# Reordering the prelude of a selective-scan layer: exponentials and logarithms by pairs of batches, all of softplus ahead of the scans, and the output bias from a product with ones

## The reference

```python
x = layernorm(x)                               # 4 x 512 x 128
gate = sigmoid(x @ W2 + b2)                    # 256 channels
u = sigmoid(causal_conv4(x @ W1 + b1) + conv_b)
xp = u @ x_proj_w                              # 64 + 16 + 16 columns
delta = softplus(xp[:, :64] @ dt_proj_w + dt_proj_b)
for each of 16 states n:                       # one recurrence over 512 tokens each
    h = exp(delta * A[n]) * h + delta * u * B[n]
    y += h * C[n]
out = (y + u * D) * gate @ Wo + bo             # added to the layer's input
```

## Time and profile before

| | |
|---|---|
| runs | 1500.18, 1506.36, 1511.74 us; median 1506.36 |
| profiled execution | 1509.37 us, of which span 1507.1 us |
| granted TensorE clock, mean | 0.883 of full speed |
| PE busy | 1237.4 us (82%) |
| DVE busy | 1035.0 us (69%) |
| ACT busy | 729.2 us (48%) |
| POOL busy | 628.0 us (42%) |
| scan layer: prelude | 0 to 72.07 us, when the first scan starts |
| scan layer: scans and tail | 72.07 to 304.81 us |

### The profile page before, as it was taken

The page is one execution under the profiler, slowest core; times in us unless marked ns, Lnnn a source line. Parts: engine busy times, 40 slices in busy tenths (PEclk is TensorE's granted clock), DMA queues, the critical chain, the costliest instruction groups (busy, mean ns, idle before and its releaser), DMA issues. The chain is left out here.

```text
span 1507.1 us, 30851 instructions
## 1 busy us (share of the span) xinstructions
PE 1237.4 (82%) x11642; PEld 673.8 (45%) x11642; DVE 1035.0 (69%) x2290; ACT 729.2 (48%) x1596; POOL 628.0 (42%) x838
## 2 busy tenths in 40 slices
PE   6656677779999988538889988988988799999976
PEld 2212232222333337424666766666666333333276
DVE  6699999979888955457446646645632588988653
ACT  3834334317766675313524523533442166676754
POOL 2279888853424215314423423223332524351244
PEclk9878888869999998758889879978997599999988
DMA  5378833023224022441421231141120231331213
GB/s 166 145 274 320 298 139 140 20 67 87 55 65 122 13 82 63 100 86 23 88 38 25 45 74 28 21 100 18 18 51 10 67 79 31 97 89 45 81 48 88
DMA packets 137737, 128.41 MB, mean 85 GB/s; under 512 B 92007, under 2 KB 123559, under 8 KB 132202
## 3 DMA queue, kind: packets, MB, share of 16 engines
q1 hardware_dynamic: 129536, 118.56, 28.6%
q0 software_dynamic: 2496, 5.13, 1.1%
q10 hardware_dynamic: 5558, 2.76, 0.9%
HBM read 105.61 MB, written 38.62 MB: 96 GB/s over the span
## 5 line engine op out<-in xcount | busy, mean ns | idle before, releaser
L1393 DVE TENSOR_REDUCE f_row_min<-f_ps 128x1 f32<-128x512 f32 x512 | 323.9, 676 | 55.6 <-PE f_ps L1720 55.2
L1283 ACT ACTIVATE f_e<-f_ps 128x512 f32<-128x512 f32 x512 | 282.8, 602 | 126.4 <-PE f_ps L1740 122.5
L1720 PE MATMUL f_ps<-f_operands 72*128 72x512 bf16 x512 | 205.4, 410 | 26.4 <-DMA f_operands<-k_scr 15.4
L1740 PE MATMUL f_ps<-f_operands 75*128 75x512 bf16 x512 | 189.5, 380 | 2.6 <-ACT f_e L1283 2.1
L790 PE MATMUL m_ps<-m_shared,sb_ident 128*128 128x512 f32 x256 | 136.8, 683 | 58.1 <-DVE m_shared L630 58.0
L363 POOL TENSOR_TENSOR m_drive<-m_du,m_ring 128x1024 f32<-128x1024 f32 x64 | 149.7, 2352 | 56.2 <-DVE m_ps L622 37.6
L495 ACT ACTIVATE m_ps<-m_delta,m_A 128x511 f32<-128x511 f32 x128 | 83.0, 681 | 131.7 <-DVE m_ps L622 109.0
L1751 PE MATMUL f_ps<-f_e,f_v_op 128*32 128x512 f32 x1024 | 136.4, 604 | 2.1 <-ACT f_e L1283 1.4
L2714 DVE TENSOR_TENSOR d_aT<-d_ps,d_aT 128x16 f32<-128x16 f32 x224 | 37.9, 169 | 140.9 <-PE d_ps L2892 140.7
L1720 PEld LDWEIGHTS f_ps<-f_operands 72*128 72x128 bf16 x512 | 51.3, 101 | 181.2 <-DVE f_row_min L1393 127.3
L2545 DVE TENSOR_REDUCE d_row_min<-d_ps 128x1 f32<-128x384 f32 (+3 forms) x176 | 106.3, 634 | 35.9 <-PE d_ps L2786 34.7
(11 more groups left out here) (298 smaller groups left out, 2345.3 us busy)
## 6 DMA issues: line engine op xcount, KB each, us to landing
m_ring<-bc_scr SPq DMA_DIRECT2D x32, 1024.0 KB, 5.4
f_rows_scr<-blank SPq DMA_DIRECT2D x2, 8707.5 KB, 30.8
f_wall<-f_wall SPq DMA_DIRECT2D x16, 578.0 KB
f_operands<-q_scr SPq DMA_DIRECT2D x32, 288.0 KB
f_operands<-k_scr SPq DMA_DIRECT2D x96, 96.0 KB
d_q_op<-q_scr SPq DMA_DIRECT2D x6, 576.0 KB
d_k_op<-k_scr SPq DMA_DIRECT2D x18, 192.0 KB
f_operands<-f_rows_scr SPq DMA_DIRECT2D x46, 64.5 KB, 1.8
```

The source lines that it names most:

```text
L1283: nc.scalar.activation(e_sb[:, n % 3, hh, :], ps[:, SCORE[(b * UNITS + u) % SCORE_BANKS], :], ACT.Exp, scale=SCALE).then_inc(s["e_out"], 1)
L1393: nc.vector.tensor_reduce(row_min[:, b % 2, u // TPB, u % TPB:u % TPB + 1], ps[:, MAXQ[(b * UNITS + u) % MAX_BANKS], :], AX.X, ALU.max, ne ...
L1720: nc.tensor.matmul(ps[:, MAXQ[n % MAX_BANKS], :], q_op(b, QK)[:, hd, t * P:(t + 1) * P], k_op(b, QK)[:, hd, :], start=True, stop=True).the ...
L1740: nc.tensor.matmul(ps[:, SCORE[n % SCORE_BANKS], :], k_op(b, QKS)[:, hd, t * P:(t + 1) * P], q_op(b, QKS)[:, hd, :], start=True, stop=True ...
```

## The change

On ACT: `steps(0)` moves in front of `gates(1)`; `inputs(2)` and `steps(1)` come next; then the exponentials of batches 0 and 1 follow each other, then their logarithms; `inputs(3)`, `steps(2)`, `gates(2)`, `gates(3)`, `steps(3)`; the exponentials of 2 and 3, and their logarithms, all ahead of the first decay. On DVE `one_plus`, and then `softplus`, run by pairs too, and those of batches 2 and 3 stand in front of the scans. On PE `project_rows(1)` moves in front of `project_u(2)`, `project_dt(0)` in front of `project_gate(1)`, and likewise for the later batches. POOL's four additions of the bias go, with `add_output`'s wait for them; instead `project_out` opens each 128 x 128 tile of the sum with a product of a row of ones and the row `m_bo` (four more matmul calls a batch), for which DVE sets `ones_row` at the start.

```diff
-                pool.wait_ge(s["rest_in"], 16 * (1 + len(later_loads(core))))
-                for b in range(B):
...
-                    nc.gpsimd.tensor_tensor(x_sb[:, tiles, :], x_sb[:, tiles, :],
-                                            row(core, "m_bo").unsqueeze(1).to_broadcast([P, TPB, H]),
-                                            ALU.add).then_inc(s["bias_out"], 1)
...
                 inputs(1)
                 turned(2)
                 raw(2)
+                steps(0)
                 gates(1)
                 turned(3)
-                steps(0)
+                inputs(2)
+                steps(1)
                 decline(0)
+                decline(1)
                 logarithm(0)
-                inputs(2)
+                logarithm(1)
                 inputs(3)
-                steps(1)
+                steps(2)
                 gates(2)
                 gates(3)
-                decline(1)
-                steps(2)
-                logarithm(1)
                 steps(3)
                 decline(2)
                 decline(3)
+                logarithm(2)
+                logarithm(3)
...
-                        if step == DEFERRED_AT + 1:
-                            for later in DEFERRED:
-                                logarithm(later)
...
                 norm(3)
+                projections(1)
                 convolve(2)
-                projections(1)
+                projections(2)
                 one_plus(0)
+                one_plus(1)
                 softplus(0)
-                projections(2)
-                one_plus(1)
+                softplus(1)
                 projections(3)
-                softplus(1)
                 dve.wait_ge(s["gate_out"], B)
...
-                for later in DEFERRED:
-                    one_plus(later)
+                one_plus(2)
+                one_plus(3)
+                softplus(2)
+                softplus(3)
...
-                    dve.wait_ge(s["bias_out"], b + 1)
...
-                    if step + 1 == DEFERRED_AT:
-                        for later in DEFERRED:
-                            softplus(later)
...
                 turn(2)
+                project_rows(1)
                 project_u(2)
+                project_dt(0)
                 project_gate(1)
-                project_dt(0)
                 turn(3)
-                project_rows(1)
+                project_dt(1)
+                project_rows(2)
                 project_u(3)
-                project_dt(1)
+                project_dt(2)
                 project_gate(2)
-                project_rows(2)
+                project_rows(3)
                 project_gate(3)
-                project_dt(2)
-                project_rows(3)
                 project_dt(3)
...
                     for t in range(TPB):
+                        here = bank(Y)[:, t * H:(t + 1) * H]
+                        nc.tensor.matmul(here, ones_row[:, :], row(core, "m_bo")[0:1, :], start=True, stop=False)
```

More of the change, by code:

```diff
@@ L217, in mamba_phase @@
         CONV_STEPS = CONV_K * HALVES
-        DEFERRED = (2, 3)
-        DEFERRED_AT = 1
         gate = sb("gate", [P, HALVES, T])
@@ L232, in mamba_phase @@
         edge_w = sb("edge_w", [CONV_K - 1, MLP])
+        ones_row = sb("ones_row", [1, P])
         PAD = S + CONV_K - 1
@@ L260, in mamba_phase @@
                  "dt_ps z_out e_out one_e_out lost_out log_out log1p_out delta_out du_out decay_zeroed decay_out drive_out "
-                 "scan_out hC_dve_out hC_pool_out y_dve y_pool yg_out o_ps bias_out x_out "
+                 "scan_out hC_dve_out hC_pool_out y_dve y_pool yg_out o_ps ones_out x_out "
                  "f_stats f_mv f_var f_rstd f_hn f_hT_ps f_hT_sb f_qk_ps f_qk_sb f_split f_stored")
@@ L346, in _ @@
                     layer_norm_rstd(nc, pool, core, ln[b % 2], s, "ln", b + 1)
-                pool.wait_ge(s["rest_in"], 16 * (1 + len(later_loads(core))))
-                for b in range(B):
-                    tiles = slice(b * TPB, (b + 1) * TPB)
-                    pool.wait_ge(s["ln_done"], b + 1)
-                    nc.gpsimd.tensor_tensor(x_sb[:, tiles, :], x_sb[:, tiles, :],
-                                            row(core, "m_bo").unsqueeze(1).to_broadcast([P, TPB, H]),
-                                            ALU.add).then_inc(s["bias_out"], 1)
                 def drive_of(step):
@@ L517, in _ @@
                 nc.vector.memset(core.minus_half[:, :], -0.5)
+                nc.vector.memset(ones_row[:, :], 1.0).then_inc(s["ones_out"], 1)
                 for i in range(2):
@@ L797, in project_out @@
                         pe.wait_ge(s["rest_in"], 16 * (1 + len(later_loads(core))))
+                        pe.wait_ge(s["ones_out"], 1)
                     for t in range(TPB):
+                        here = bank(Y)[:, t * H:(t + 1) * H]
+                        nc.tensor.matmul(here, ones_row[:, :], row(core, "m_bo")[0:1, :], start=True, stop=False)
                         for k in range(HALVES):
-                            last = nc.tensor.matmul(bank(Y)[:, t * H:(t + 1) * H], yg[:, k, t * P:(t + 1) * P],
-                                                    Wo[:, k, :], start=(k == 0), stop=(k == HALVES - 1))
+                            last = nc.tensor.matmul(here, yg[:, k, t * P:(t + 1) * P], Wo[:, k, :], start=False, stop=(k == HALVES - 1))
                     last.then_inc(s["o_ps"], 1)
```

## The result

The changed kernel takes 1514.9 us (median of 20 runs, 1506.4 to 1522.1) against 1507.2 for the kernel before in 20 runs: ratio 1.0053, 95% interval 1.0036 to 1.0069. It is 8 us slower. I had forecast 1 us faster, and the range ended at 1511.

What follows compares the result with a forecast made beforehand. It took DVE as the bound from the first scan on, and a chain of hand-overs before it. Earlier scans -2.6, wait at first gating +0.6, product with ones +1.0: -1.0 us, 1505.3 against 1506.4; range 1498.5 to 1511.

Steps and rivals of the forecast that it cites:

- the product with ones: Bias added on PE by four more calls a batch: 1.0 us a batch, added whole only in the last batch.
- For batches 0 to 2 it is hidden: In these batches the longer product costs nothing, since `add_output` comes 4.8 us after the product ends.
- The ladder of the prelude: Six timed stages before the scans: scan 0 starts at 80.0, scan 2 at 85.7 in place of 88.29, 2.6 us gained.
- rival A's second half: PE at full clock at `project_dt(3)`, before 3.05 us: prelude 1.1 us shorter, 1500.6 with both halves; whole rival's chance 0.25.
- Step 4: In the prelude, `softplus(1)` on DVE takes turns with POOL's first four drives: 52.2 to 60.5 in place of 56.0.
- Step 2: In the prelude, POOL adds no bias: `norm(3)` ends at 32.6, not 35.49, `convolve(2)` at 38.9, not 41.25; gain 2.4.
- Chunk 8: Ring chunk on SP's queue behind the first blank copy: lands at 122.6 in place of 115.7; POOL waits 3.0 before drive 16.
- The wait at the gating: DVE's first gating, `gated(0)`, due at 132.9, waits 0.6 us for PE's sums, which end at 133.5.
- rival B's sign: A pause of DVE before `gated(0)` of over 2 us.
- Rival B: Slower: the ring chunk behind the blank copy lands 2 to 6 us later than 122.6, giving 1507 to 1511; chance 0.15.
- The sum: Whole kernel: -2.6 + 0.6 + 1.0 = -1.0 us, with the layer's end at about 304.
- the named slower rivals: Late ring chunk, 1507 to 1511, chance 0.15; PE losing its clock in the prelude, 1509, chance 0.05.

Runs made afterwards that it cites:

- e7b_ones_k64: The changed kernel with the product with ones over 64 rows in place of one; a single execution, only its trace read: last product 5.8 us.

## Why the prediction was wrong, point by point

**The step that failed is the product with ones.** "Four calls more are 1.0 us a batch if a contraction over one row costs what one over 128 does (the nearest row; the bounds are 0 and, at the half clock seen elsewhere, 2.0)". The sum for 128 rows was right: that run's last product took 2.94 us, 0.9 over 2.05. For one row the batch took 4.3 more than 2.05, not 1.0. Two things that I had not priced make the other 3.4: about 0.4 us a tile at the full clock for the changes between unlike numbers of rows (1.4 a batch, from the batch with 64 rows at the full clock), and the clock, which falls while PE works and slows the old sixteen instructions too (2.1). My upper bound took the half clock for the new instructions alone.

**"For batches 0 to 2 it is hidden"** failed for batch 2. I compared the product's end with `add_output` only. Behind it on PE stand the two products that make q and k of the next layer, ACT waits for them in its list, and its decays wait behind: 2.15 and 0.51 us of idle DVE. With 128 rows only the 0.51 is left.

**The ladder of the prelude held.** Scan 0 was to start at 80.0 and scan 2 at 85.7; it was 78.77 and 84.47. Of the 1.2 us, 1.1 are rival A's second half, the clock at `project_dt(3)`: 1.98 us, not 3.05. Step 4, the turns, held: `softplus(1)` took 7.8 us (52.42 to 60.22) where I had 8.3, and the run with later drives took 4.1 of them away. Step 2's bias off POOL is worth 2.9 in the new order and nothing in the old.

**Chunk 8** landed at 122.6 (93.82 and 28.8), the time that I had, but by luck: the blank copy was issued 1.2 us earlier than forecast (88.54), took 31.8 us in place of 30.3, and chunk 8 came 2.3 behind it. POOL, ready earlier too, paused 4.2, not 3.0. The wait at the gating was 3.5, not 0.6: the scans were 1.2 us ahead of my ladder and only waited for it, and the sums ahead of it ran partly at the lower clock (131 to 133 us at 0.63 and 0.50; 5.40 us where eight sums at the full clock take 3.70), which took them to 135.23 in place of 133.5. In six like runs where the clock held in these sums the wait was 1.0 to 1.4 us. So rival B's sign came, a pause of over 2 us, but not its cause: the chunk was on time. Rival B itself came in `e7b_ones_k64`: the blank copy took 33.3 us, chunk 8 landed at 124.8, and the gating waited 3.50 us with the clock at 1.00.

**The sum.** Against my forecast the layer ends 7.0 us late (310.84 for 303.8): 1.8 at the first gating (135.27 for 133.5), 3.3 in the last product beyond its 1.0, 2.6 in batch 3, and -0.7 at the two gatings between.

**The rivals' chances.** I gave the named slower rivals 0.2 in all, and none of it to the one part of the change that was new on the chip. I took the range for an operation that the trace did not show from rows of another shape, and gave it no rival. The trace of the kernel before had a nearer row, in the prelude, at the full clock:

```profile
41.28 0.38 PE L711 MATMUL m_ps<-sb_m_edge,m_edge_w 3*128 3x3 f32 x2
41.59 3.70 PE L710 MATMUL m_ps<-m_shared 128*128 128x512 f32 x8
```

Two instructions over 3 rows and with 3 columns each, among products over 128 rows, take 0.31 us from start to start (41.28 to 41.59), 0.16 an instruction, where one with 128 columns takes 0.13. Priced by its columns this would be close to nothing. It does not show the clock's fall.

What stays open: whether it is the weights' load or the product itself that can't run on across a change of rows, and why the clock falls in some batches with a one-row or 64-row product and not in others. No run takes them apart.

## What to carry to other kernels

A product of a new shape is not priced by its columns: between products over 128 rows, each one over 1, 32 or 64 cost 0.4 us here beyond its own time, and in most batches the clock went down for what came behind. Where a bias must go through PE, repeat it over all rows, which cost 0.9 us a batch here, or give it to an engine at a time when it is idle, which cost 0.2 us at most (scan 2 at 84.68 against 84.47). When a product gets longer, look for all that stands behind it in PE's list, not only for who waits for its result.

## What the runs showed of the hardware

TensorE's clock fell to the half level in the middle of unbroken work, 1.5 to 2.6 us after products over one row began among those over 128, in all four batches of the changed kernel; with 32 rows it did so in all four batches too, with 64 in three of four, and with 128 rows, in the same number and place, it stayed at 1.00. In the kernel before the clock fell in unbroken work as well (238.7 us, 1.2 us after PE resumed), but never in the product with Wo.

A group of two instructions over 1, 32 or 64 rows and four over 128 took 1.05 us at the full clock, and 0.67 with 128 rows throughout. The trace of the kernel before has no product of 128 columns over one, 32 or 64 rows.
